# Attention over heads in fp32: the probabilities' block transfers on ScalarE's own queue, and another order for the first three tiles

## The reference

```python
n = layernorm(x)                                     # over 512
Q, K, V = (n @ W.T + b).reshape(tokens, 16, 32)      # three projections
a = softmax(Q K^T / sqrt(32)); o = a V               # per token, 16x16
o = o.transpose(batch, head, token, d).reshape(batch, 2048, 512)
x1 = x + layernorm(o @ Wo.T + bo)
out = x1 + layernorm(layernorm(layernorm(x1)) * ln_g + ln_b)
```

## Time and profile before

| | |
|---|---|
| three runs | 1796.73, 1800.51, 1801.62 us; median 1800.51 |
| the profiled execution | 1804.97 us, of it the span 1803.2 us |
| mean granted TensorE clock | 0.983 of full speed |
| busy | PE 93%, DVE 73%, POOL 71%, ACT 49% of the span |
| DMA | 294.77 MB, mean 163 GB/s |
| chain of work that ended last | PE 90% |

### The profile page before, as it was taken

How to read it: one execution, slowest core, us unless ns; L and a number is a source line. 1 busy time by engine, 2 the same in 40 slices (tenths; PEclk the granted TensorE clock), 3 DMA queues, 4 the chain that set the end, 5 groups by cost and what they waited for, 6 DMA issues and landing times.

```text
span 1803.2 us, 55394 instructions
## 1 busy us (share of the span) xinstructions
PE 1685.1 (93%) x22528; PEld 1338.3 (74%) x22528; DVE 1310.0 (73%) x2440; ACT 877.2 (49%) x1736; POOL 1279.2 (71%) x1293
## 2 busy tenths in 40 slices
PE   3999999999999999999999999999999999999992
PEld 2777777777777777777777777777777777777771
DVE  5577767767778778777777677677678777777764
ACT  3344545445545454544544454455445454445443
POOL 4467767677777777777677677677677777677756
PEclk9999999999999999999999999999999999999996
DMA  6566666666667666666666566666667666667651
GB/s 239 137 152 165 163 163 175 156 164 169 166 164 178 161 175 171 167 168 172 163 168 170 152 165 176 156 162 182 154 167 177 161 168 164 160 163 178 155 135 58
DMA packets 388918, 294.77 MB, mean 163 GB/s; under 512 B 297140, under 2 KB 297140, under 8 KB 388151
## 3 DMA queue, kind: packets, MB, share of 16 engines
q1 hardware_dynamic: 370230, 257.66, 57.9%
q10 hardware_dynamic: 18432, 33.56, 5.1%
HBM read 156.77 MB, written 67.24 MB: 124 GB/s over the span
## 4 chain that ended last, share of the span: by engine, by line
PE 90%; issue 4%; DVE 2%; DMA 1%; POOL 1%; ACT 1%; SPq 1%; POOLq 0%; ACTq 0%; DVEq 0%
PE ps_k L591 21%; PE ps_v L591 19%; PE ps_q L591 19%; PE ps_y L655 19%; PE ps_o L623 6%; PE ps_s L607 5%; SPq L235 1%; DMA x_d<-mr 0%; DMA p_bd<-pT 0%; POOL z L343 0%; SPq L246 0%; ACT z L510 0%; POOL o_sb L358 0%; DVE z L495 0%; DMA x_in<-in_xa 0%
## 5 line engine op out<-in xcount | busy, mean ns | idle before, releaser
L343 POOL TENSOR_TENSOR z<-z,b_row 128x512 f32<-128x512 f32 x128 | 193.1, 1528 | 251.4 <-DVE z L495 251.4
L495 DVE TENSOR_TENSOR z<-z,g_row 128x512 f32<-128x512 f32 x128 | 88.6, 692 | 236.3 <-ACT z L510 235.4
L323 POOL TENSOR_TENSOR probs<-probs,inv 128x512 f32<-128x512 f32 x128 | 136.0, 1063 | 169.9 <-DVE inv L446 169.9
L563 ACT ACTIVATE q_sb<-ps_q,mr 128x512 f32<-128x512 f32 x128 | 88.2, 689 | 332.0 <-PE ps_q L591 332.0
L567 ACT ACTIVATE v_tok<-ps_v,mr 128x512 f32<-128x512 f32 x128 | 88.1, 688 | 270.2 <-PE ps_v L591 270.2
L287 POOL TENSOR_TENSOR x_t<-x_t,mr_row 128x512 f32<-128x512 f32 x128 | 201.1, 1571 | 17.1 <-DMA mr_row<-x_d 16.7
L591 PE MATMUL ps_k<-wk_hi,xT_hi 128*128 128x512 f32 x512 | 159.4, 434 | 26.0 <-POOL xT_lo L293 26.0
L623 PE MATMUL ps_o<-p_bd,v_key 64*32 64x64 f32 x8192 | 120.3, 226 | 58.0 <-issue 54.5
L293 POOL TENSOR_TENSOR xT_lo<-x_t,xT_hi 128x512 fp32r<-128x512 f32 x128 | 165.9, 1296 | 4.2 <-ACT xT_hi L519 4.2
L358 POOL TENSOR_TENSOR o_sb<-o_sb,x 128x512 f32<-128x512 f32 x128 | 161.2, 1281 | 6.4 <-ACT o_sb L510 6.1
L352 POOL TENSOR_TENSOR x<-x,res 128x512 f32<-128x512 f32 x128 | 162.8, 1294 | 0.5 <-ACT x L510 0.5
(11 more groups left out here) (81 smaller groups left out, 3828.7 us busy)
## 6 DMA issues: line engine op xcount, KB each, us to landing
x_t<-in_xt SPq DMA_DIRECT2D x64, 512.0 KB
res<-in_xr SPq DMA_DIRECT2D x64, 512.0 KB, 4.3
k_bd<-kT SPq DMA_DIRECT2D x512, 64.0 KB, 2.0
v_d<-v_tok ACTq DMA_DIRECT2D x128, 256.0 KB, 2.7
v_key<-v_d SPq DMA_DIRECT2D x128, 256.0 KB, 5.5
p_bd<-pT SPq DMA_DIRECT2D x512, 64.0 KB, 2.0
out<-o_sb SPq DMA_DIRECT2D x64, 512.0 KB, 4.3
x_in<-in_xa SPq DMA_DIRECT2D x63, 512.0 KB, 6.2
```

Source lines behind the costliest of these rows:

```text
L323: nc.gpsimd.tensor_tensor(probs[t % 2][:, :, :, :].rearrange("p i u k -> p (i u) k"), probs[t % 2][:, :, :, :].rearrange("p i u k -> p (i ...
L343: nc.gpsimd.tensor_tensor(z[:, j, :], z[:, j, :], b_row[:, :], ALU.add).then_inc(z_done, 1)
```

## The change

The four p_bd transfers of a tile leave SP's queue and are issued by ScalarE on its own queue, between q_sb and v_tok of the same slot. The store and the load of pair 0's roots move to ScalarE too, ahead of the first cast. In the first slots the order changes on all engines: GpSimd takes the low part of tile 0 ahead of centring tile 1, VectorE transposes tile 0's keys after the low part of wq and takes the statistics of pair 1 ahead of slot 0, the cast and the low part of wo come later, and TensorE projects tile 0 as soon as each third of its operands is there, takes the keys of tile 1 ahead of the scores of tile 0, and the keys of tile 2 ahead of the mixing of tile 0. From slot 3 on, TensorE's order is as before.

```diff
@@ SyncE: at the start, and in a slot
-                if k == "v":
-                    load_mr(0)
...
-                if k == "q":
-                    store_mr(0)
...
-                t = s - 1
-                if tile(t):
-                    sp.wait_ge(pT_done, t + 1)
-                    if t >= 2:
-                        sp.wait_ge(o_ready, t - 1)
-                    else:
-                        sp.wait_ge(p_zeroed, 1)
-                    for c in range(4):
-                        rows = slice(32 * c, 32 * c + 32)
-                        sp.dma_start(p_bd[rows, t % 2, c % 2, :], pT[t % 2][rows, :, :].rearrange("p n h -> p (n h)")
-                                     ).then_inc(p_moved[t % 2], DMA)
@@ GpSimd: at the start
             x_centre(0)
+            x_low(0)
             x_centre(1)
-            x_low(0)
@@ VectorE: at the start, and in slots 0 and 1
             low(1, "q", wq_hi, wq_lo)
+            k_turn(0)
             low(2, "v", wv_hi, wv_lo)
+            x_moments(1)
+            q_turn(0)
...
-                if s % 2 == 0 and 1 <= v < NV:
+                if s % 2 == 0 and 2 <= v < NV:
                     x_moments(v)
...
-                if s == 0:
+                if s == 1:
                     low(3, "o", wo_hi, wo_lo)
@@ ScalarE: at the start, and in a slot
+            act.wait_ge(root_done["X"], 1)
+            nc.scalar.dma_start(x_d[0], mr[0][:, 0:2, :].rearrange("p k j -> p (k j)")).then_inc(mr_stored[0], DMA)
+            act.wait_ge(mr_stored[0], DMA)
+            nc.scalar.dma_start(mr_row[0][:, :, :, :].rearrange("p n k j -> p (n k j)"),
+                                x_d[0].rearrange("(a p) q -> a (p q)", a=1).broadcast_to([P, 4 * P])).then_inc(mr_loaded[0], DMA)
             cast(0, "k", wk_hi)
             x_high(0)
...
-                if s == 0:
-                    cast(3, "o", wo_hi)
...
                     nc.scalar.activation(q_sb[:, :], ps_q[:, :], ACT.Copy, scale=r[:, 3, t % 2:t % 2 + 1]).then_inc(q_put, 1)
+                t = s - 1
+                if tile(t):
+                    act.wait_ge(pT_done, t + 1)
+                    if t >= 2:
+                        act.wait_ge(o_ready, t - 1)
+                    else:
+                        act.wait_ge(p_zeroed, 1)
+                    for c in range(4):
+                        rows = slice(32 * c, 32 * c + 32)
+                        nc.scalar.dma_start(p_bd[rows, t % 2, c % 2, :], pT[t % 2][rows, :, :].rearrange("p n h -> p (n h)")
+                                            ).then_inc(p_moved[t % 2], DMA)
+                t = s
+                if tile(t):
                     act.wait_ge(v_ready, t + 1)
...
                     nc.scalar.dma_start(v_d[t % 2], v_tok[t % 2][:, :]).then_inc(v_stored[t % 2], DMA)
+                if s == 0:
+                    cast(3, "o", wo_hi)
@@ TensorE: the waits of tile 0 inside project, and the order (keys, queries, ... are the parts of a slot as before)
+                for i, (x, w) in enumerate(((x_hi, w_hi), (x_lo, w_hi), (x_hi, w_lo))):
+                    if t == 0:
+                        if i == 0:
+                            pe.wait_ge(xhi_done, 1)
+                            pe.wait_ge(w_cast, n)
+                        elif i == 1:
+                            pe.wait_ge(xlo_done, 1)
+                        else:
+                            pe.wait_ge(w_split, n)
...
+            for s in range(NT + 2):
+                if s == 1:
+                    keys(1)
+                if 0 <= s - 1 < NT:
+                    scores(s - 1)
+                if s == 2:
+                    keys(2)
+                if 0 <= s - 2 < NT:
+                    mixed(s - 2)
+                if s < NT:
+                    if s not in (1, 2):
+                        keys(s)
+                    queries(s)
+                    values(s)
+                if 0 <= s - 2 < NT:
+                    output(s - 2)
```

More of the change, by code:

```diff
@@ L389, in low, with k_turn, q_turn @@
                 nc.vector.tensor_tensor(lo[:, :, :], raw[k], hi[:, :, :].bitcast(F32), ALU.subtract).then_inc(w_split, 1)
+            def k_turn(t):
+                dve.wait_ge(k_ready, t + 1)
+                if t >= 2:
+                    dve.wait_ge(k_moved[t % 2], 4 * DMA * (t // 2))
+                nc.vector.transpose(kT[t % 2][:, :, :].rearrange("p n h -> p h n"),
+                                    ps_k[:, :].rearrange("p (h d) -> p h d", d=D)).then_inc(kT_done, 1)
+            def q_turn(t):
+                dve.wait_ge(q_put, t + 1)
+                if t >= 2:
+                    dve.wait_ge(s_ready, t - 1)
+                nc.vector.transpose(qT[t % 2][:, :, :].rearrange("p n h -> p h n"),
+                                    q_sb[:, :].rearrange("p (h d) -> p h d", d=D)).then_inc(qT_done, 1)
             x_moments(0)
@@ L448, in _ @@
                 t = s
[L449 to L454, removed]
+                if 1 <= t < NT:
+                    k_turn(t)
                 t = s - 1
@@ L479, in _ @@
                 v = (s + 4) // 2
-                if s % 2 == 0 and 1 <= v < NV:
+                if s % 2 == 0 and 2 <= v < NV:
                     x_moments(v)
                 t = s
[L483 to L488, removed]
-                if s == 0:
+                if 1 <= t < NT:
+                    q_turn(t)
+                if s == 1:
                     low(3, "o", wo_hi, wo_lo)
@@ L590, in project @@
                     for e in range(EC):
-                        mm = nc.tensor.matmul(ps[:, :], x[:, e, :], w[:, e, :], start=x is x_hi and w is w_hi and e == 0,
-                                              stop=w is w_lo and e == EC - 1)
+                        mm = nc.tensor.matmul(ps[:, :], x[:, e, :], w[:, e, :], start=i == 0 and e == 0,
+                                              stop=i == 2 and e == EC - 1)
                 mm.then_inc(ready, 1)
[L595 to L628, removed]
-                    pe.wait_ge(xlo_done, t + 1)
[L630 to L657, removed]
@@ new lines, in keys, with queries, values @@
+            def keys(t):
+                if t:
+                    pe.wait_ge(xlo_done, t + 1)
+                    pe.wait_ge(kT_done, t)
+                project(t, 1, ps_k, wk_hi, wk_lo, k_ready)
+            def queries(t):
+                if t:
+                    pe.wait_ge(q_put, t)
+                project(t, 2, ps_q, wq_hi, wq_lo, q_ready)
+            def values(t):
+                if t:
+                    pe.wait_ge(vtok_done, t)
+                project(t, 3, ps_v, wv_hi, wv_lo, v_ready)
@@ new lines, in scores @@
+            def scores(t):
+                pe.wait_ge(qT_done, t + 1)
+                pe.wait_ge(k_moved[t % 2], 4 * DMA * (t // 2 + 1))
+                if t:
+                    pe.wait_ge(sub_done, t)
+                for a in range(4):
+                    for c in range(4):
+                        n = 8 * a + 2 * c
+                        for r in range(2):
+                            half = slice(64 * r, 64 * r + 64)
+                            mm = nc.tensor.matmul(ps_s[32 * c:32 * c + 32, r, a * 64:a * 64 + 64],
+                                                  qT[t % 2][half, n:n + 2, :].rearrange("p n h -> p (n h)"),
+                                                  k_bd[half, t % 2, :, n * H:n * H + 32], start=True, stop=True,
+                                                  tile_position=(64 * r, 32 * c), skip_group_check=True)
+                mm.then_inc(s_ready, 1)
@@ new lines, in mixed @@
+            def mixed(t):
+                pe.wait_ge(v_moved[t % 2], DMA * (t // 2 + 1))
+                pe.wait_ge(p_moved[t % 2], 4 * DMA * (t // 2 + 1))
+                if t:
+                    pe.wait_ge(olo_done, t)
+                for a in range(4):
+                    for g in range(4):
+                        n = 8 * (g // 2) + 2 * a + g % 2
+                        for r in range(2):
+                            half = slice(64 * r, 64 * r + 64)
+                            mm = nc.tensor.matmul(ps_o[32 * g:32 * g + 32, r, a * 64:a * 64 + 64],
+                                                  v_key[t % 2][half, 4 * g + a, :], p_bd[half, t % 2, :, 32 * n:32 * n + 32],
+                                                  start=True, stop=True, tile_position=(64 * r, 32 * g), skip_group_check=True)
+                mm.then_inc(o_ready, 1)
@@ new lines, in output @@
+            def output(t):
+                pe.wait_ge(olo_done, t + 1)
+                if t:
+                    pe.wait_ge(y_done, t)
+                else:
+                    pe.wait_ge(w_split, 4)
+                o_hi, o_lo = oT_hi[t % 2], oT_lo[t % 2]
+                for i, (o, w) in enumerate(((o_hi, wo_hi), (o_lo, wo_hi), (o_hi, wo_lo))):
+                    for a in range(EC):
+                        mm = nc.tensor.matmul(ps_y[:, :], o[:, a, :], w[:, a, :], start=i == 0 and a == 0,
```

(2 more changed lines are left out.)

4 lines of the change are left out of this document (2 added, 2 removed).

## The result

The changed kernel takes 1831.62 us (median of 4 runs, 1829.17 to 1835.99) against 1801.07 for the kernel before in the same set: a ratio of **1.0178**, 95% interval 1.0152 to 1.0203. It is slower by 1.8%; the forecast was 3.3% faster. The profiled execution took 1835.99, its span is 1834.3.

What follows compares the result with a forecast made beforehand. TensorE's matmuls were taken as the bound, with 86 us lost over 125 slots. Gains of 48 (waits) + 8 (clock) + 3.5 (start) - 0.4 (end) = 59 took 1800.5 to 1741 us, own range 1730 to 1753; wider range 1724 to 1776.

Steps and rivals of the forecast that it cites:

- Removed from SP: SP's queue loses 2.43 us a slot; x loads go 2.5 earlier in odd slots, costing 0 to 1.6 each, taken as 0.
- start as now: Odd slots: q_sb ends at 828.18, so p_bd's issue starts no earlier on ScalarE; nothing gained or lost.
- 58 less 10: Waits before the mixing: 58 us could go by issuing p_bd 1.3 earlier in even slots; 10 kept for landings of 4.1.
- Half of it: Rival, 1774 us, chance 0.16: earlier x loads slow p_bd by 2.1 in odd slots, 38 us of waits.
- The two queues take turns: Rival, 1797 us, chance 0.08: SP's issuing holds ScalarE back, so only the start's 3 us are gained.
- Slower: Rival, 1866 us, chance 0.04: ScalarE's issues delay the queries, scores start 2.0 late in 62 slots, 125 us lost.
- 8 of 10 us of clock: Low-clock pieces follow waits near 2 us; with those gone 8 us return, bounds 0 to 10.
- 3.5 of the start: First tiles: pair 0's roots on ScalarE's queue and the new order end tile 0's output projection 3.5 us earlier (0 to 8).
- 18 to 23 of halts: Halts inside the mixed block: 5 us taken from PE's listed waits, and another 13 to 18 of the lost 86.
- a landing over 3.5 in the odd slots: Sign of being wrong: p_bd's landing in the odd slots passes 3.5 us.
- halts in place of waits: Sign of being wrong: halts inside the mixed block grow in place of the waits before it.

Runs made afterwards that it cites:

- gated: Changed kernel, but SP waits for p_bd to land before the store of roots, the loads of x and the residual load: 1753.00 us, ratio 0.9805.
- one_load_gated: Changed kernel, but in odd slots the second load of x (x_in) waits for p_bd's landing while x_t goes out early: 1787.03 us, ratio 0.9985.
- small_x: Changed kernel with the two loads of x in the slots cut to 16 of 1024 values a partition: 1765.70 us, ratio 0.9878.
- gate_odd: Changed kernel with SP's wait for p_bd's landing in the odd slots alone: 1779.98 us, ratio 0.9950.
- gate_old_start: Kernel before with p_bd issued by ScalarE and SP waiting for p_bd's landing ahead of its big loads, old start kept: 1756.75 us, ratio 0.9803.
- gate_roots_sp: Changed kernel with SP's wait for p_bd in all slots, and pair 0's roots stored and loaded by SP again: 1755.58 us, ratio 0.9806.

## Why the prediction was wrong

**The step that failed** is "Removed from SP": "So contention costs p_bd between nothing and 3.1 us in the odd slots, where it has 1.5 to spare: 0 to 1.6 for each of 63 slots. I take 0". Measured, the landing there went from 2.02 to 5.51, that is by 3.5, above the upper bound too, and the wait it makes is 87.6 / 62 = 1.4 in each such slot. By p_bd's own rows: the fourth issue starts 1.85 after the first, 1.85 + 5.51 = 7.36, against 6.09 to the due time: 1.27. That this is inside the 0 to 1.6 named for each slot owes something to luck: the issue doesn't "start as now", it starts 5.43 ahead of the scores instead of 4.66, so the transfers had 2.2 to spare and not 1.5. The bound of 3.1 came from the store of the roots, which is issued ahead of the loads; 0 was chosen by landings in slots in which no load stood beside them. In the kernel before, the order of SP's queue kept p_bd ahead of the slot's 512 KB loads, so its 2.0 to 2.5 was a property of that order and not of the transfer. That is what the change took away.

**A part of the same step was missing.** The paragraph counts what comes earlier in the odd slots alone. In the even slots the residual load, 512 KB, comes up behind k_bd too. p_bd lands there in 4.01 instead of 2.38. The gain expected there, 58 less 10 (measured waits before: 58.7, of them 53.7 in the even slots), came to 37.1. That it came so near has luck in it too: two misses offset each other, a landing 1.6 later that was left out, and an issue that starts 2.45 earlier (5.43 ahead of the scores instead of 2.98) where 1.3 was expected.

**The rivals.** "Half of it" had the mechanism and the place, but priced the landing at 2.1 more instead of 3.5, and 38 us for the odd slots instead of 82.6; with 82.6 in it, and the even slots' 16.6 of waits, it would have been on the slow side (58 - 82.6 - 16.6 + 3 + 3.5 - 0.4 = 35 us lost). "The two queues take turns" fell: p_bd's issue starts while k_bd is still being issued, and k_bd's four issues take 2.54 beside p_bd's 2.46 in the even slot shown, 2.42 and 2.43 alone. The Trainium skill ("Perfetto Trace Analysis", section "DMA Instruction — HWDGE (DVE, Sync)") has two issuing sequencers share one descriptor generator, locked while it generates; in two streams side by side no turn longer than these 0.1 us shows. How long such a lock lasts within one issue, no run here tells. "Slower" by ScalarE's issues fell as well: v_tok still waits 2.11 to 2.12 for ps_v and isn't 0.36 late, as p_bd's issue starts 0.06 behind q_sb's start, runs beside it and costs ScalarE nothing.

**Clock and start.** 8 of 10 us of clock and 3.5 of the start were to come back. The granted clock of the stretch stayed at 0.99 with waits of up to 3.1 left, and rose to 1.00 in gated, where they are gone. The start gave nothing: on ScalarE's queue the store of the roots needs 7.06 and the load 5.88, in the chain after, against 7.50 and 3.26:

```profile
7.56 7.06 DMA x_d<-mr
14.64 5.88 DMA mr_row<-x_d
```

It is the same fault a second time: "on ScalarE's queue the store takes between 1.4 and 4.5" took another queue for a way round the traffic of the weights. Whether it is the weights' loads that hold it up there wasn't tried.

**What was right:** the 58 us of waits before the mixing (measured 58.7) and the 18 to 23 of halts (measured 18.4); the even slots' cause; that the issues cost ScalarE nothing; and, with the crossing taken away, the slot of 13.11 (I expected 13.0 to 13.1) and the range: 0.9805 of 1800.5 is 1765, inside 1724 to 1776. That it isn't 1741 lies in part in the halts, which grow from 18.4 to 30.4 when the waits go, and in the start's 3.5; the rest of the 24 us can't be followed, as the kernel before ran at 1783.85 in that set and its only profile took 1804.97. I had named both signs of being wrong that came, a landing over 3.5 in the odd slots and halts in place of waits; the price of the first was in reach and not taken.

## What to carry to other kernels

A queue's order is also a rule about which transfers fly together. Before a small, urgent transfer leaves a queue, write down which large loads behind it come earlier by that, and price its landing beside them, not by its landing in the old order. Where the issue does gain from a queue of its own, hold the large loads back until the urgent one has landed: one wait turned +1.8% into -2.0% here.

## What the runs showed of the hardware

A 64 KB transfer that lands in 2.0 us alone lands in 4.0 beside one 512 KB load on the other queue (even slots), 4.85 and 5.5 beside one and two of the odd slots' loads (medians of after and one_load_gated; 2.0 are the medians of gated). The profile's packets show the form: 3 us in which 94 packets of one queue start and none of the other, then both. The Trainium skill ("DMA: Bandwidth & Descriptors", section "Queues, rings and completion order") says that each DMA engine takes turns between queues only after a whole packet, of some 9 to 17 descriptors. A 512 KB load here is 128 pieces of 4096 bytes (what the profile counts as packets), 8 for each of 16 engines, so by that page (an estimate) one load fits into one turn. The trace agrees with that: in the odd slot shown, 111 of the 128 pieces of x_t have started when ScalarE's queue gets on at 853, and in the even slot shown 104 of the residual load's when it gets on at 838.5.

The first pieces of such a load take long by their records: 16 pieces of x_t 1.5 to 2.4 us each in the odd slot shown, 8 of the residual load's 1.0 to 1.2 us in the even one, and almost nothing else starts meanwhile (14 packets in 2 us). This pause lies inside p_bd's delay, but the crossing doesn't make it: the longest piece of a load of x takes 1.95 us in gated and 2.04 in the kernel after (medians). What it is, no run here tells.

The halts inside the mixed block, about 1 us each, are of two kinds. Those of the tiles whose p_bd is issued in odd slots go with the loads of x (18.5 in gated, 0.0 in small_x, with no waits before the block in either). Those of the other tiles are 11.9 to 12.6 in gated, gate_odd, gate_old_start and gate_roots_sp, the four with the gate in odd slots and the usual order, and 1.8 or less in all the others. Both go when the keys' projection stands between the two blocks of small matmuls. What feeds them stays open.
